# Perceiver layer on one core: mask, bias of y and softmax sums of the attention moved off VectorE, four exponential buffers, five low parts per half on POOL

## What is computed

```python
x = x + xattn(layernorm(x), ctx, ctx)   # 16 heads of 8; out = layernorm(o @ Wo.T + bo) * gamma + beta
x = x + attn(layernorm(x))              # one head of 128, causal, softmax(QK / sqrt(128)) V, @ Wo.T + bo
x = x + ffn(layernorm(x))               # shared MLP + top 2 of 8 experts, 128 -> 512 -> 128, silu
```

## Time and profile before

| | |
|---|---|
| median of 3 runs | 639.18 us (636.12 to 643.11) |
| profiled execution | 641.12 us, of it a span of 639.4 us |
| granted clock of PE, mean | 0.86 |
| busy over the span | PE 76%, DVE 74%, ACT 63%, POOL 53% |
| attention pipeline | from the start to about 445 us |

### The profile page before, as it was taken

The page is one execution under the profiler, slowest core; times in us unless marked ns, Lnnn a source line. Parts: engine busy times, 40 slices in busy tenths (PEclk is TensorE's granted clock), DMA queues, the critical chain, the costliest instruction groups (busy, mean ns, idle before and its releaser), DMA issues.

```text
span 639.4 us, 18314 instructions
## 1 busy us (share of the span) xinstructions
PE 482.9 (76%) x5674; PEld 404.9 (63%) x5674; DVE 471.1 (74%) x1416; ACT 400.9 (63%) x767; POOL 337.8 (53%) x486
## 2 busy tenths in 40 slices
PE   4498788777877687776876775646669999999961
PEld 1277677666766576665765664544448888888840
DVE  3259898899899989986878779675576666666744
ACT  2157677666767676653656654445669888888850
...
DMA packets 166704, 61.09 MB, mean 96 GB/s; under 512 B 116548, under 2 KB 163416, under 8 KB 166629
## 3 DMA queue, kind: packets, MB, share of 16 engines
...
...
## 4 chain that ended last, share of the span: by engine, by line
PE 39%; DVE 22%; issue 16%; POOL 10%; ACT 5%; DMA 2%; SPq 2%; DVEq 1%; POOLq 0%; ACTq 0%
PE bank L1305 8%; PE bank L1318 7%; DVE p_lo L354 3%; DVE O_tok L884 3%; PE bank L1244 2%; DVE x1n L802 2%; POOL results L615 2%; PE bank L1263 2%; PE bank L1249 2%; PE bank L1175 2%; PE bank L1157 2%; DVE m_bf L899 2%; POOL rstd L524 2%; PE bank L1282 2%; PE bank L1176 2%
## 5 line engine op out<-in xcount | busy, mean ns | idle before, releaser
L899 DVE TENSOR_REDUCE m_bf<-bank 128x4 bf16<-128x512 f32 x128 | 87.1, 681 | 32.6 <-PE bank L1263 31.1
L678 ACT ACTIVATE p<-bank 128x512 f32<-128x512 f32 x128 | 76.2, 595 | 54.8 <-POOL p_lo L354 24.7
L988 DVE TENSOR_TENSOR h_lo<-h,h_hi 128x512 f16<-128x512 f32 x112 | 77.3, 692 | 41.9 <-ACT h_hi L743 41.5
L1318 PE MATMUL bank<-W_hi,h_hi 128*128 (+1 forms) x448 | 83.0, 222 | 13.6 <-DVE h_lo L988 13.6
L354 POOL TENSOR_TENSOR p_lo<-p,p_hi 128x512 f16<-128x512 f32 x48 | 57.3, 1195 | 64.7 <-ACT p_hi L683 64.4
L615 POOL DMA_INDIRECT results<-y_sb,row_info x80 | 79.1, 989 | 19.6 <-issue 17.3
L535 POOL DMA_INDIRECT listed<-rows_of,row_no x64 | 64.9, 1014 | 38.3 <-DVE row_no L872 22.9
L683 ACT ACTIVATE p_hi<-p 128x512 f16<-128x512 f32 x128 | 80.6, 630 | 5.5
L1318 PE MATMUL bank<-W_lo,h_hi 128*128 (+1 forms) x448 | 82.5, 222 | 0.0
L1318 PE MATMUL bank<-W_hi,h_lo 128*128 (+1 forms) x448 | 82.5, 222 | 0.0
L740 ACT ACTIVATE h<-bank 128x512 f32<-128x512 f32 x112 | 66.8, 596 | 22.7 <-PE bank L1305 18.7
(11 more groups left out here) (195 smaller groups left out, 1356.5 us busy)
## 6 DMA issues: line engine op xcount, KB each, us to landing
...
Ks<-k_rows SPq DMA_DIRECT2D x128, 64.0 KB
...
Qs<-q_rows SPq DMA_DIRECT2D x128, 32.0 KB
...
```

The lines of the kernel that those rows point to most:

```text
L678: act.activation(p32[:, s % 2, :], T_ps[s % 2][:, :], ACT.Exp, scale=XSCALE).then_inc(exp_done, 1)
L899: dve.tensor_reduce(m_bf[:, slot, :], M_ps[s % 2][:, :].rearrange("p (n k) -> p n k", k=SK), AX.X, ALU.max).then_inc(max_done, 1)
L988: dve.tensor_tensor(h_lo[k % RING][:, :], h32[k % RING][:, :], h_hi[k % RING][:, :], ALU.subtract).then_inc(hlo_done, 1)
L1318: last = pe.matmul(y[:, t * D:t * D + D], hh[k % RING][:, cols], ww[:, w(c)], start=(first and c == 0 and t == 0 and m == 0), stop=(end an ...
```

## The change

- The mask: the queries are scaled by -1/sqrt(128) at their evacuation, so s holds the negated scores, and PE adds +1e30 at masked places with one more product (`neg_ident` with a bf16 mask of -1e30). DVE needs one operation, a minimum, whose result is the bias of the exponential. `sm`, `smax` and L917 go.
- The row sums: V2 gets a column of ones, so z has the sum in its column 129; `accum_out` goes; the reciprocal is taken from z.
- The bias of the self-attention output is added to V2 (its softmax sums to one) in its evacuation, which DVE does now in place of ACT; `x1b` goes.
- The bias of y: three bf16 parts of it, each multiplied with a row of ones by PE. `yb` goes, statistics and normalisation read PSUM.
- s and y get a bank of their own, 3, which is taken from the maxima: `M_ps` has one bank. PE's product of unit u+2 waits for the reduce of u+1.
- `normalise_values` does both tiles in one reciprocal and two multiplications.
- `p32` has four buffers; `ON_POOL` = 1, 2, 3, 6, 7.
- `normalise` is a scalar_tensor_tensor with rstd as a broadcast tensor. The memsets before the statistics go. DVE's steps are all written out. Five small chained operations on DVE for the three parts of the bias join the setup, with two others (the scaled query bias, the bf16 copy of the mask); PE waits for them before unit 0.

```diff
-        ("v2", 1, -2, 0), ("s", 1, -2, 1),
+        ("v2", 1, -2, 0), ("s", 1, -2, 2),
-        ("ctxT", 3, 2, 0), ("y", 3, -1, 1),
+        ("ctxT", 3, 2, 0), ("y", 3, -1, 2),
-ON_POOL = (1, 4, 6)
+ON_POOL = (1, 2, 3, 6, 7)
...
-        p32 = asb("p32", [P, 2, 512])
+        p32 = asb("p32", [P, 4, 512])
-        M_ps = bank[2:4]
+        M_ps = bank[2]
-        X_ps = bank[6:8]
+        X_ps = (bank[6], bank[7], bank[3])
-        W_ps = bank[2:6]
+        W_ps = (bank[2], bank[4], bank[5], bank[0])
...
-                        pool.wait_ge(x1_done, h)
-                        pool.tensor_tensor(x1b[1 - r][:, :, :], x1[1 - r][:, :, :],
-                                           bcast[:, 1:2, :].broadcast_to([P, 2, D]), ALU.add).then_inc(x1b_done, 1)
...
-                        hl, sl = (h, s - 2) if s > 1 else (h - 1, s + UNITS - 2)
+                        hl, sl = (h, s - 4) if s > 3 else (h - 1, s + UNITS - 4)
...
+                    if s == 2 and valid(c):
+                        act.wait_ge(nbias_done, c + 1)
+                        need(act, mm["pT"], c)
+                        for t in range(2):
+                            act.activation(P2[:, t, :], XB["s"][:, t * P:t * P + P], ACT.Exp, bias=nbias[:, t:t + 1],
+                                           scale=-1.0).then_inc(p2_done, 1)
...
+                dve.wait_ge(setup_dve, 3)
+                dve.tensor_copy(bias_parts[:, 0, :], bcast[0:1, 0, :]).then_inc(setup_dve, 1)
+                dve.wait_ge(setup_dve, 6)
+                dve.tensor_tensor(bias_rest[:, 0, :], bcast[0:1, 0, :], bias_parts[:, 0, :], ALU.subtract).then_inc(setup_dve, 1)
...
-                dve.memset(scratch[:, 2 * i:2 * i + 1], 0.0)
...
-                    dve.tensor_scalar(dst[:, t, :], src[:, t, :], mv[:, i, t, 0:1], rstd[:, i, t:t + 1],
-                                      ALU.subtract, ALU.mult).then_inc(normed[n], 1)
+                    dve.scalar_tensor_tensor(dst[:, t, :], src[:, t, :], mv[:, i, t, 0:1],
+                                             rstd[:, i, t:t + 1].broadcast_to([P, D]),
+                                             ALU.subtract, ALU.mult).then_inc(normed[n], 1)
...
+                        dve.tensor_reduce(nbias[:, :], XB["s"][:, 0:2 * P].rearrange("p (t k) -> p t k", k=P),
+                                          AX.X, ALU.min).then_inc(nbias_done, 1)
+                    if s == 2 and valid(c):
+                        dve.wait_ge(mm["v2"], c + 1)
+                        need(dve, mm["z"], c)
+                        dve.tensor_tensor(V2[:, :, 0:D], XB["v2"][:, 0:2 * P].rearrange("p (t d) -> p t d", d=D),
+                                          bcast[:, 1:2, :].broadcast_to([P, 2, D]), ALU.add).then_inc(ev["v2"], 1)
...
+                    for n in range(3):
+                        last = pe.matmul(x[:, 0:2 * D].rearrange("p (t d) -> p t d", d=D), ones_bf[:, :],
+                                         bias_parts[:, n:n + 1, :].broadcast_to([1, 2, D]), start=False, stop=(n == 2))
...
+                    last = pe.matmul(x[:, 0:2 * P].rearrange("p (t k) -> p t k", k=P), neg_ident[:, :],
+                                     causal_bf[:, :].unsqueeze(1).broadcast_to([P, 2, P]), start=False, stop=True)
...
-                        need(pe, max_done, u + 1)
+                        need(pe, max_done, u + 2)
```

More of the change, by code:

```diff
@@ L218, in perceiver @@
         x1 = [asb(f"x1_{r}", [P, 2, D]) for r in range(2)]
-        x1b = [asb(f"x1b_{r}", [P, 2, D]) for r in range(2)]
         x1n = asb("x1n", [P, 2, D])
@@ L246, in perceiver, with ps @@
         k_rows = nc.dram_tensor("k_rows", (2, HL, P, HL, CB * SK), F16).ap()
-        bank = [es.enter_context(nc.psum_tensor(f"bank{n}", [P, 512], F32)) for n in range(8)]
+        def ps(name, width):
+            return es.enter_context(nc.psum_tensor(name, [P, width], F32))
+        bank = [ps(f"bank{n}", 512) for n in range(4)]
+        pairs = ps("pairs", 2 * 512)
+        bank += [pairs[:, 0:512], pairs[:, 512:1024]] + [ps(f"bank{n}", 512) for n in range(6, 8)]
         T_ps = bank[0:2]
-        M_ps = bank[2:4]
+        M_ps = bank[2]
         PV_ps = bank[4:6]
-        X_ps = bank[6:8]
+        X_ps = (bank[6], bank[7], bank[3])
         XB = {n: X_ps[b] for n, _, _, b in MISC}
-        W_ps = bank[2:6]
+        W_ps = (bank[2], bank[4], bank[5], bank[0])
         G_ps = X_ps[0]
@@ L313, in half_cols, with all_steps @@
             return slice(2 * P * h, 2 * P * (h + 1)) if isinstance(h, int) else bass.ds(h * (2 * P), 2 * P)
+        def all_steps(step, setup):
+            for h in range(FIRST, HALVES + 2):
+                if h == 0:
+                    setup()
+                step(h, h % 2)
         def most_steps(eng, step, setup):
@@ L689, in step @@
                         need(act, mm["s"], c)
-                        act.activation(QT[:, :], XB["qk"][:, 0:2 * P], ACT.Identity, bias=col("abq"))
+                        act.activation(QT[:, :], XB["qk"][:, 0:2 * P], ACT.Identity, bias=abq_scaled[:, :], scale=-ASCALE)
                         act.activation(KT[:, :], XB["qk"][:, 2 * P:4 * P], ACT.Identity, bias=col("abk")).then_inc(ev["qk"], 1)
-                    if s == 1 and valid(c):
-                        need(act, mm["z"], c)
-                        evacuate("v2", c, V2[:, :, :], XB["v2"][:, 0:2 * P])
                     if s == 2 and valid(f):
@@ L705, in step @@
                         evacuate("ctxT", f, cT[r][:, :], XB["ctxT"][:, :])
-                    if s == 3 and valid(c):
-                        act.wait_ge(nbias_done, c + 1)
-                        need(act, mm["pT"], c)
-                        for t in range(2):
-                            act.activation(P2[:, t, :], sm[:, t, :], ACT.Exp, bias=nbias[:, t:t + 1], scale=ASCALE,
-                                           accum_out=rs[:, t:t + 1]).then_inc(p2_done, 1)
                     if s == 3 and valid(d):
@@ L777, in setup @@
                 dve.scalar_tensor_tensor(gate_lo[:, :], gateT, WSCALE, gate_hi[:, :], ALU.mult, ALU.subtract).then_inc(gate_split, 1)
+                bq = ROWS.index("abq")
+                dve.tensor_scalar(abq_scaled[:, :], vec[:, bq:bq + 1], -ASCALE, None, ALU.mult).then_inc(setup_dve, 1)
                 dve.wait_ge(setup_ev, 4)
@@ L883, in normalise_tile @@
                     rows_ = slice(S * o, S * o + S)
-                    last = dve.tensor_tensor(O_tok[rows_, p, :, :], pv[rows_, :, HD * o:HD * o + HD],
-                                             rden[rows_, p, :].unsqueeze(2).broadcast_to([S, HEADS, HD]), ALU.mult)
+                    last = dve.tensor_tensor(O_tok[rows_, :, :, :], pv[rows_, :, :, HD * o:HD * o + HD],
+                                             rden[rows_, :, :].unsqueeze(3).broadcast_to([S, PAIRS, HEADS, HD]), ALU.mult)
                 last.then_inc(norm_done, 1)
@@ L903, in step @@
                         low_part(dve, hb, back)
+                    if s == 1 and valid(b):
+                        normalise_values(b)
                     if s == 1 and valid(c):
@@ L941, in step @@
                                                  k_parts[:, 0, :], ALU.add, ALU.subtract).then_inc(ev["k"], 1)
-                    if s == 4 and valid(c):
-                        dve.wait_ge(p2_done, 2 * c + 2)
-                        need(dve, x2_done, 2 * c)
-                        dve.reciprocal(rrs[:, :], rs[:, :]).then_inc(rrs_done, 1)
                     if s == 5 and valid(a):
@@ L1034, in shared_before @@
                         shared_out(n // CH - 1)
-            most_steps(dve, step, setup)
+            all_steps(step, setup)
             shared_before(0, EARLY * CH)
@@ L1182, in shared_bank @@
                     for t in range(2):
[L1183 to L1184 removed]
+                        pe.matmul(x[:, t * P:t * P + P], QT[:, t * P:t * P + P], KT[:, t * P:t * P + P],
+                                  start=(t == 0), stop=False)
+                    last = pe.matmul(x[:, 0:2 * P].rearrange("p (t k) -> p t k", k=P), neg_ident[:, :],
+                                     causal_bf[:, :].unsqueeze(1).broadcast_to([P, 2, P]), start=False, stop=True)
                 if name == "pT":
@@ L1192, in shared_bank @@
                     for t in range(2):
-                        last = pe.matmul(x[:, t * D:t * D + D], P2T[:, t * P:t * P + P], V2[:, t, :], start=True, stop=True)
+                        last = pe.matmul(x[:, t * (D + 1):(t + 1) * (D + 1)], P2T[:, t * P:t * P + P], V2[:, t, :],
+                                         start=True, stop=True)
                 last.then_inc(mm[name], 1)
```

96 lines of the change are left out of this document (47 added, 49 removed).

## The result

The changed kernel takes 652.93 us (median of 4 runs, 651.57 to 654.53) beside 640.66 for the kernel before (4 runs, 636.12 to 643.11): ratio 1.020, 95% interval 1.013 to 1.027. It is slower beyond the scatter, by 1.3 to 2.7%. Predicted were 615 us and a range of 600 to 633, so the forecast has the wrong sign. The profiled execution took 651.64 us, with a span of 649.9.

The account below looks back on a forecast made before the run. DVE, nearly full, in a loop with PE was taken as the bound. Terms -16.3 (nine halves), -3.6, -3.0, -1.8, -1 and +1.5 sum to -24.2: profiled 641.1 becomes 617, or 615 us as median; range 600 to 633.

Parts of the forecast that it names:

- Step C: Unit 3's reduce to q_parts' end: shorter block saves 1.43 us, V2's evacuation on DVE adds 0.34; net -1.09 a half.
- DVE's load: Per half, DVE's 19.5 us falls by 1.4 (two p_lo), 1.4 (block) and 0.7 (x1n), so 19.9 us fits.
- Step A: V_lo to PE's transpose of x1n, 4.54 us: removing x1b saves 0.74; the collision with unit 6's p_lo stays.
- Step B: Transpose of x1n to unit 3's reduce, 4.61 us: single maxima bank counted 0, up to 0.69 per binding step.
- Rival 4: Single maxima bank makes product and reduce alternate: a half 2.8 us longer before the gain, 655 us; chance 0.08.
- Step D: From ctxT to the next V_lo, 6.29 us: counted 0, between -0.7 and +1.2.
- Setup: Before PE starts unit 0: seven more short DVE operations, mostly chained, add 1.5 us (0.4 to 2.9).
- Memsets, four buffers, unrolled loop: Removed statistics memsets, four exponential buffers and DVE's written-out loop: each counted 0, being off the path or in idle time.
- Sending stretch: Halves while POOL sends rows: POOL is the floor, 23.0 us a half against 24.2; three such halves -3.6.
- Rival 1: x1n is freed from POOL's collision too, 0.5 to 1.2 us a half; 607 us with 0.5; chance 0.12.
- Rival 3: POOL's slower p_lo and longer queue make yn about 1.2 us late every half; 634 us; chance 0.14.
- The ports shared by DVE and POOL: At x1n: the new two-SBUF-input form stays blocked by POOL; if only 2-port mode collided, x1n would gain 0.5 us.

Follow-up runs that it names:

- experiment 1: Changed kernel with DVE's V2 evacuation in slot 1, before the O_tok multiplications, instead of slot 2: 653.11 us, ratio 1.017.
- experiment 9: experiment 1 with unit 2's low part back on DVE (POOL has units 1, 3, 6, 7): 628.68 us, ratio 0.981.
- experiment 4: experiment 1 with units 1, 4, 6 on POOL instead of 1, 2, 3, 6, 7: 625.05 us, ratio 0.973.
- experiment 8: experiment 4 with units 1, 3, 4 on POOL and POOL's addition xb moved to slot 1 of the next step: 617.76 us, ratio 0.965.
- experiment 11: experiment 8 with POOL's addition xb back in slot 7, right behind the root of x1: 619.23 us, ratio 0.963.
- experiment 12: experiment 8 with unit 3's low part back on DVE (POOL has units 1, 4): 612.59 us, ratio 0.955.
- experiment 7: experiment 1 with normalise as tensor_scalar again instead of scalar_tensor_tensor: 648.03 us, ratio 1.010.
- experiment 10: experiment 4 with unit 2 added on POOL (units 1, 2, 4, 6): 647.06 us, ratio 1.006.
- experiment 5: Changed kernel with units 1, 4, 6 on POOL, V2 staying in slot 2: 649.7 us, ratio 1.015.
- experiment 3: Kernel before with one bank for the maxima, PE waiting for the reduce of unit u+1: 646.97 us, ratio 1.007.
- experiment 2: Kernel before with V2 copied by DVE in slot 2 instead of by ACT in slot 1: 673.78 us, ratio 1.047.
- experiment 6: experiment 4 with two buffers for the fp32 exponentials instead of four: 626.48 us, ratio 0.978.

## Why 24 to 28 us hang on half a microsecond

The x2n collision costs 0.5 us a half where it stands, yet experiments 1 and 9 differ by 1.5 us a half in the eight halves from the fourth V_lo on. The windows of single halves show the rest, first two of experiment 1, then one of experiment 9 (the granted clock is the third number from the end):

```profile
87.53:109.04 21.51, 17.48 (x227) 14.33 (x225) 18.27 (x48) 14.69 (x29) 11.53 (x16) 0.92 0.42 88
152.78:177.46 24.68, 20.76 (x227) 16.47 (x225) 18.40 (x48) 14.57 (x29) 11.43 (x16) 0.79 0.36 88
```

```profile
108.03:128.73 20.70, 17.57 (x227) 14.61 (x225) 18.37 (x48) 14.49 (x29) 10.70 (x15) 0.92 0.49 102
```

All three hold the same number of PE's instructions (227 and 225). At a clock of 0.92 the half takes 21.51 us and 20.70; at 0.79 it takes 24.68. Single microseconds of that slow half:

```profile
155.78:156.78 1.00, 0.06 (x3) 0.00 (x0) 1.00 (x2) 0.00 (x0) 1.00 (x2) 1.00 0.31 64
157.78:158.78 1.00, 0.90 (x7) 0.74 (x8) 1.00 (x4) 0.38 (x1) 0.45 (x1) 0.50 0.47 94
...
164.78:165.78 1.00, 0.59 (x8) 0.59 (x8) 0.97 (x3) 0.89 (x3) 0.92 (x3) 1.00 0.24 37
...
166.78:167.78 1.00, 0.48 (x19) 0.38 (x16) 1.00 (x3) 0.97 (x2) 0.32 (x1) 1.00 0.89 215
167.78:168.78 1.00, 0.74 (x4) 0.75 (x5) 0.72 (x2) 0.05 (x1) 0.88 (x1) 0.58 0.52 155
...
173.78:174.78 1.00, 1.00 (x5) 0.56 (x4) 0.00 (x0) 0.30 (x1) 0.78 (x2) 0.50 0.00 0
```

The clock falls twice, from 1.00 (2.4 GHz) to 0.50 (1.2 GHz): once after PE has idled for x1n (busy 0.06 of the microsecond from 155.78), which happens in nearly every half of every version, and again after the idle around O_tok and q_parts (0.59 and 0.48), where it stays low up to 174.78. In experiments 4, 8, 9, 11 and 12, where PE idles 0.5 to 0.6 us in the 4.5 us around the transpose of O_tok, the second fall is in none of the eight halves after the fourth V_lo; in experiment 1 (1.0 us idle) it is in two, in experiments 7 and 10 (1.0) in three, in experiment 5 (1.5) in two, in experiment 3 (1.7) in four, in experiment 2 (1.4) in seven. It is not each gap that does it: the kernel before idles 1.8 us there and the changed one 1.5, and each has the second fall once; the changed one has a longer first one instead, 4.7 us at the lower level a half for 3.4.

The mean length of the eight halves that follow the fourth V_lo, of those among them that ran at a clock of 0.92, and the four halves behind them (to the sixteenth V_lo: the routing and the sending of rows) together:

| kernel | all eight, us | at 0.92, us (count) | next four together, us |
|---|---|---|---|
| before | 21.89 | 21.71 (5) | 108.0 |
| changed | 22.66 | 21.96 (4) | 106.0 |
| experiment 1: V2 early | 22.38 | 21.46 (4) | 113.3 |
| experiment 5: units 1, 4, 6 | 23.05 | 21.95 (2) | 104.4 |
| experiment 10: V2 early, 1, 2, 4, 6 | 22.70 | 21.45 (3) | 106.7 |
| experiment 4: V2 early, 1, 4, 6 | 20.93 | 20.76 (7) | 98.0 |
| experiment 9: V2 early, 1, 3, 6, 7 | 20.93 | 20.78 (7) | 98.6 |
| experiment 12 | 20.26 | 20.50 (6) | 93.8 |

At one clock the kernels order themselves by what holds PE: 21.95 as long as V2 is late, whichever units POOL has; 21.46 with V2 early and unit 2 on POOL, where PE waits for q_parts instead; 20.77 with both cured. So V2 early alone does gain 0.5 a half. The remainder, 0.2 in experiment 4 and 0.9 in experiment 1, goes with the clock.

The last column shows why experiment 1 took as long as the changed kernel. Up to the twelfth V_lo it is 6.0 us ahead; in the next four halves it loses 7.3. The first sending half, in the changed kernel, experiment 1 and experiment 4:

```profile
305.02:332.80 27.78, 20.60 (x234) 17.64 (x235) 22.96 (x55) 14.93 (x29) 19.95 (x24) 0.82 0.30 69
```

```profile
301.01:331.08 30.07, 23.98 (x234) 19.61 (x235) 22.25 (x55) 14.97 (x29) 19.85 (x24) 0.66 0.27 66
```

```profile
287.57:309.42 21.85, 18.36 (x234) 15.48 (x235) 19.80 (x56) 14.82 (x29) 15.92 (x21) 0.92 0.37 84
```

PE's instructions are the same in number, the clock is 0.82, 0.66 and 0.92. Of the 28 us between experiments 1 and 4 the eight halves give 11.6, these four 15.3 and the rest 1.9, so more than half of the effect lies where rows are sent. How much of it there is clock and how much POOL's longer queue is not separated. That PE's idle time brings the clock down is read from where it fell in these rows; no run set the clock by itself. The Trainium skill ("TensorE: Matmul & The Clock Gate", HAM oscillation) describes a loop in which each wait is followed by products at half the clock; the 0.50 rows agree with that. The waits there are for DMA, here for DVE.

## Why the prediction failed, step by step

- **Step C, the one that set the sign.** It priced V2's evacuation at 0.34 of DVE's time and said that ACT's lighter load was off the path. The cost was a new wait, PE's q product on V2: 15.8 us in eight waits, 25.3 in all the attention. Reading the bank table would have shown it: the evacuation releases bank 6 for q. The question that the step never asked was who waits for the moved instruction. The block itself was priced well: 1.62 for 1.46. In total C, from the reduce to the end of q_parts, was 5.76 and is 265.37 + 0.48 - 260.11 = 5.74; forecast 4.67. V2 early alone did not turn the result (653.11); with the second omission cured as well it is 625.05, faster than before.
- **Step C, second omission.** It moved low parts to POOL and looked for the price on POOL's side. x2n lies between the reduce and q_parts and was not checked for a neighbour: its pair went from two of 339 ns to 1.13 us. Experiments 9 and 10 put 24 and 22 us on this one unit, once V2 is early.
- **DVE's load.** The sum had it fall by 1.4 + 1.4 + 0.7 = 3.5 a half and called that room enough. It fell by 1.2: x1n's 0.7 did not come, x2n's pair took 0.6 more, and V2's 0.4, which C had booked, was missing in that sum.
- **Step A.** Booked -0.74 for `x1b`. A went from 4.54 to 255.26 - 250.78 = 4.48 (the transpose of x1n starts at 255.26), forecast 3.80. x1n's pair went from 1.81 to 1.92, since the low part moved up by just what `x1b` had taken and `xb` moved up behind it. The step saw that collision and left it in, but took the addition as a term beside it; whatever POOL has behind the root is one block that x1n waits out. The gain was to be had from the order on POOL: in experiment 8, 0.61.
- **Step B.** Booked 0, up to 0.69 where it binds. PE waits for the reduce 8.2 us, ten times, 0.9 a half; experiment 3 prices the bank at 4 us or so. Rival 4 had the mechanism at 2.8 us a half; experiment 3's halves grew by 0.4 (22.26 for 21.89).
- **Step D.** Booked 0; 6.29 became 272.56 - 266.15 = 6.41. DVE waits longer for y (10.7 us before its statistics in the eight halves), which takes up the time of the low part that left; yn from PSUM costs what was thought.
- **Setup** +1.5: the second V_lo starts at 51.57 for 49.85, +1.7. **Memsets, four buffers, unrolled loop** at 0: experiment 6 bears out the buffers; the other two were not tried alone.
- **Sending stretch** -1.2 a half: nothing came, 24.5 us a half. The floor of 23.0 assumed that POOL could be kept busy; it waits as before for DVE and PE, at a clock of 0.83, and is busy 78.83 of 104 us, not over 90%. In experiment 12, with two low parts on POOL, the three halves take 63.3 us together.
- **The clock** was no term. The forecast took the granted clock of before (0.91) as given; its fall to 0.88 in the eight halves is worth about 0.5 us of the 0.77 by which a mean half grew, the other 0.25 being the difference at 0.92.
- **The rivals.** None was right. Rival 4 named 655 us and has the right sign, but its mechanism gave some 4 us of the 12, so that its number is close is luck. Rival 1 named the gain on x1n that experiment 8 later found. Rival 3's wait of yn for rstd is 3.3 us in all.
- **The ports shared by DVE and POOL.** The Trainium skill ("SBUF — State Buffer", two separate sides) says that a DVE operation with two SBUF inputs or in a 2-port mode and a GpSimd operation that reads SBUF exclude each other, and that the one that starts first holds the ports to its end. The prediction used the rule for x1n only. Experiments 7 to 9 agree with it: both forms of the normalisation are held where POOL's operation started first, and x2n's pair falls from 1.14 to 0.61 us without POOL's low part beside it. The rule of the Trainium skill ("VectorE: DVE Perf Modes", perf-mode tier table) that fp32 tensor_scalar in SBUF has twice the rate (its figures are for 2048 elements a row, here it is 128) does not show: yn, xn and x2n took 341, 332 and 339 ns by tensor_scalar before, and xn and x2n 343 and 348 by scalar_tensor_tensor in experiment 4, where unit 2 is off POOL.

What stays open: why a late V2 leaves the first fall of the clock longer in the changed kernel; why experiment 1 ran its first sending half at a clock of 0.66; and the last 3 us at the start (the halves before the fourth V_lo), which went away with V2 early but were not tested alone.
